# Softplus of three batches: the rounding of 1 + w taken over one VectorE instruction in SBUF

## The chip, the cores and the metric

The kernel runs on one core of one Trainium2 chip. The metric is the device time of one execution in microseconds; every time below is in microseconds unless it is marked ns. The engines are named as in the profile: PE is TensorE's matrix multiply and PEld its weight load, DVE is VectorE, ACT is ScalarE, POOL is GpSimd, SP is SyncE, which here only issues DMAs.

## The reference

One block of a network: half a mixture-of-experts layer, a state-space layer, half a mixture-of-experts layer again, each behind a layer norm and added to its input. The change lies in the state-space layer:

```python
x_proj = x @ W_x.T                                  # x is the normed input, (4, 512, 256)
dt_x, Bm, Cm = jnp.split(x_proj, [R, R + N], axis=-1)
dt = jax.nn.softplus(dt_x @ W_dt.T + b_dt)
A = -jnp.exp(A_log)
dA = jnp.exp(jnp.einsum('bld,dn->bldn', dt, A))
dBx = jnp.einsum('bld,bln,bld->bldn', dt, Bm, x)
# scan over l: h = dA * h + dBx;  y = sum over n of h * C;  then y + x * D
```

All in float32, N = 16 states for each of 4 batches, 512 positions, 256 channels. The softplus of z is computed as max(z, 0) + log1p(w) with w = exp(-|z|). The kernel gets log1p(w) as ln(1 + w) + (w - ((1 + w) - 1)): the second term gives back what the rounding of 1 + w lost.

## The kernel before

Channels lie on the partitions in two blocks (k = 0, 1) and positions along the free axis, so a batch's dt is 128 x 2 x 512. The state-space layer is 64 steps of one state each (s = 16b + n, batch b and state n), and a step uses every engine once:

- ACT (`decay`, line 583, and `outer`, line 597): two exponentials of dt times a number, 128 x 511 each, into `da`, and that part of the outer product dt x B (128 x 256 for each quarter of the positions) that DVE does not do. `BY_DVE` says how many of the four quarters are DVE's: in batch 0 2 2 2 1 1 2 2 2 1 2 1 1 0 1 0 1 for n = 0 to 15, in batches 1 and 2 1 1 2 1 1 2 2 2 0 0 0 1 0 1 0 1.
- PE (`turn_dbx`, line 940): eight transposes into a pair of PSUM banks.
- DVE (`scan`, line 1317): one scan over 1,024 elements. Its inputs are `da` in SBUF and the PSUM pair. DVE's part of `outer` (line 1301) for state n + 2 stands ahead of scan n; its inputs are `dtx_t` in SBUF and B in PSUM.
- POOL (line 455): the product of the state `hs` and the broadcast row `c_sb`, both in SBUF, 1,024 elements, into one of two buffers `gs`. PE (`add`, line 956) then sums it into PSUM. POOL waits for the scan of its state and for the sum of the state two before.

The order on each engine is written out by hand; there is no planner. Each engine has its own queue and goes through it in order, and counting semaphores join them. ACT runs three steps ahead (`AHEAD`), over four buffers of `da` and `hs` (`RING`): `decay` of state s waits for scan s - 4.

The projection and softplus of batch b + 1 are spread between the steps of batch b. PE makes z in one PSUM bank T. ACT takes Abs and Relu of it with the bias (lines 565 and 566: `w_exp` and `dt_sb`), Exp of -|z| over both blocks (`project_exp`, line 570) and Ln of 1 + w (`project_ln`, line 577) into `log_w`, which is the tile `tt`. DVE computes for each block k the rounding (`project_w`: line 1272 makes (w + 1) - 1 in T, line 1274 makes w minus that in T) and then the sum (`project_dt`: line 1280 adds `log_w` and T into T, line 1282 adds `dt_sb` and T into `dt_sb`). In each pair the second instruction waits for the first. These pairs stand behind the scans n = 5, 6, 7 and 8 of batches 1 and 2, and behind n = 6, 7, 8 and 9 of batch 0, in the order w0, dt0, w1, dt1. Once both dt are there, PE transposes dt (line 925) and DVE multiplies it by x (`project_dtx`, line 1288, behind n = 10 and 12, one later in batch 0).

Behind its steps n = 5 to 8 of batches 1 and 2 (6 to 9 of batch 0) POOL also normalises one tile of 128 x 256 each (line 403, input in SBUF), and in step 3 (5 in batch 0) it makes the reciprocal deviations (lines 388, 389).

The first batch's softplus runs before the scan loop. It writes into two banks of its own, and the change leaves its arithmetic and order as they are. So the changed softplus is that of batches 1, 2 and 3, which lies in the scans of batches 0, 1 and 2.

Of the kernel before, what the change touches and what calls it, by code (L numbers as in the profile page):

```python
# [15 lines left out]
ALU = mybir.AluOpType  # L16
ACT = mybir.ActivationFunctionType
# [10 lines left out]
def macaron_kernel(nc, x, w_xT, w_dtT, b_dt, a_log, d_skip, router_w, gate_w, up_w, down_w,  # L28
# [42 lines left out]
    with ExitStack() as ctx:  # L71
# [3 lines left out]
        def sem(name):  # L75
            return ctx.enter_context(nc.semaphore(name))
# [142 lines left out]
        back_in = [sem(f"back_in{b}") for b in range(BATCH)]  # L219
        back_x = sem("back_x")  # L220
        a_ready = sem("a_ready")
        pj_all, pj_copy, pj_bt, pj_btc, pj_z, pj_abs, pj_max, pj_exp, pj_w, pj_rest, pj_ln, pj_sum, pj_dt, pj_tp, pj_dtx = (
            sem(f"pj_{s}") for s in ("all", "copy", "bt", "btc", "z", "abs", "max", "exp", "w", "rest", "ln", "sum", "dt", "tp",
                                     "dtx"))
        c_rows = sem("c_rows")
        c_in = [sem(f"c_in{u}") for u in range(RING)]
# [262 lines left out]
        def _(act):  # L489
# [71 lines left out]
            def project_abs(b, k):  # L561
                act.wait_ge(pj_z, KC * b + k + 1)
                if b > 0:
                    act.wait_ge(pj_rest, KC * b)
                nc.scalar.activation(w_exp[:, k], pj_bank(b, k), ACT.Abs, bias=b_sb[:, k:k + 1]).then_inc(pj_abs, 1)
                nc.scalar.activation(dt_sb[:, k, seq(b)], pj_bank(b, k), ACT.Relu, bias=b_sb[:, k:k + 1]).then_inc(pj_max, 1)

            def project_exp(b):
                act.wait_ge(pj_abs, KC * (b + 1))
                nc.scalar.activation(w_exp[:], w_exp[:], ACT.Exp, scale=-1.0).then_inc(pj_exp, 1)  # L570

            def project_ln(b):

                act.wait_ge(pj_exp, b + 1)
                if b > 0:
                    act.wait_ge(pj_sum, KC * b)
                nc.scalar.activation(log_w, w_exp[:], ACT.Ln, bias=1.0).then_inc(pj_ln, 1)

            def decay(s):
                if s >= RING:  # L580
# [32 lines left out]
            def scan(b):  # L613
                more = b + 1 < BATCH
                for n in range(N):
                    if b == 0 and n in (3, 4):
                        project_abs(1, n - 3)
                    if b == 0 and n == 4:
                        project_exp(1)
                    if b == 0 and n == 6:  # L620
                        project_ln(1)
                    if N * b + n + AHEAD < STATES:
                        ahead(N * b + n + AHEAD)
                    if not more and n - 1 in PIECES:
                        tanh_piece(PIECES.index(n - 1))
                    if b < 2 and n == 0:
                        ln_copy(1, 5 + b)
                    if b == 1 and n == 1:
                        ln_copy(1, 7)
                    if (b, n) in ((0, 1), (2, 0)):  # L630
                        project_copy(b + 1)
                    late = (2, 1, 0, 0)[b]
                    if 0 < b < BATCH - 1 and n in (1 + late, 2 + late):
                        project_abs(b + 1, n - 1 - late)
                    if 0 < b < BATCH - 1 and n == 3 + late:
                        project_exp(b + 1)
                    if 0 < b < BATCH - 1 and n == 4 + late:
                        project_ln(b + 1)
                    if b == 0 and n == 15:
                        project_copy(2)  # L640
                    if not more and 6 <= n < 6 + LT:
                        normalise(b - 1, n - 6)
                    turn = 13 if more else 10
                    if b > 0 and n in (turn, turn + 1):
                        ln_copy(2, 2 * (b - 1) + n - turn)
# [422 lines left out]
        def _(dve):  # L1068
# [196 lines left out]
            def project_w(b, k):  # L1265

                if k == 0:
                    dve.wait_ge(pj_exp, b + 1)
                    dve.wait_ge(pj_max, KC * (b + 1))
                elif b > 0:  # L1270
                    dve.wait_ge(pj_dt, KC * b + 1)
                nc.vector.tensor_scalar(pj_bank(b, k), w_exp[:, k], 1.0, -1.0, ALU.add, ALU.add).then_inc(pj_w, 1)
                dve.wait_ge(pj_w, KC * b + k + 1)
                nc.vector.tensor_tensor(pj_bank(b, k), w_exp[:, k], pj_bank(b, k), ALU.subtract).then_inc(pj_rest, 1)

            def project_dt(b, k):

                dve.wait_ge(pj_ln, b + 1)
                dve.wait_ge(pj_rest, KC * b + k + 1)
                nc.vector.tensor_tensor(pj_bank(b, k), log_w[:, k], pj_bank(b, k), ALU.add).then_inc(pj_sum, 1)  # L1280
                dve.wait_ge(pj_sum, KC * b + k + 1)
                nc.vector.tensor_tensor(dt_sb[:, k, seq(b)], pj_bank(b, k), dt_sb[:, k, seq(b)], ALU.add).then_inc(pj_dt, 1)

            def project_dtx(b, h):

# [18 lines left out]
            def scan(b):  # L1304
                more = b + 1 < BATCH
                for n in range(N):
                    s = N * b + n
                    if s + 2 < STATES:
                        outer(s + 2)
                    dve.wait_ge(sc_dbx, s + 1)  # L1310
                    dve.wait_ge(sc_da, KC * (s + 1))
                    if s >= RING:
                        dve.wait_ge(sc_g, s - RING + 1)
                    if s == 0:
                        dve.wait_ge(da_zero, 1)
                    flat = "p k t -> p (k t)"
                    nc.vector.tensor_tensor_scan(hs[:, s % RING].rearrange(flat), da[:, s % RING].rearrange(flat),  # L1317
                                                 DBX[s % 2][:, :, :].rearrange(flat), 0.0, ALU.mult, ALU.add).then_inc(sc_h, 1)
                    if b == 0 and n in (1, 2):
                        shared_result(0, 3, (n - 1,))  # L1320
                    if b == 0 and n == 5:
                        dve.wait_ge(back_x, BATCH)
                        stats_of(1, BATCH - 1)
                    if not more and n - 2 in PIECES:
                        hidden_piece(PIECES.index(n - 2))
                    if b > 0 and n == 1:
                        add_y(b - 1)
                    if b > 0 and n == 2:
                        dve.wait_ge(sc_x, KC * b)
                        stats_of(2, b - 1)  # L1330
                    if more and n == 4:
                        project_bt(b + 1)
                    late = int(b == 0)
                    if more and n in (5 + late, 7 + late):
                        project_w(b + 1, (n - 5) // 2)
                    if more and n in (6 + late, 8 + late):
                        project_dt(b + 1, (n - 6) // 2)
                    if more and n in (10 + late, 12 + late):
                        project_dtx(b + 1, (n - 10) // 2)

# [106 lines left out]
```

## Time and profile before

| | |
|---|---|
| median of 3 runs | 451.88 (450.79 to 455.43) |
| span of the profiled execution, first to last instruction | 460.6 |
| its granted TensorE clock, mean | 0.979 |
| DVE busy | 366.0 (79%), 600 instructions |
| ACT busy | 284.4 (62%), 537 instructions |
| POOL busy | 281.2 (61%), 215 instructions |
| PE busy | 392.2 (85%), 2540 instructions |
| first and last scan start | 145.4 and 339.3 |

The profile gives no time of the profiled execution other than its span; that is 8.7 longer than the median of the runs without a profile, and so is not one of them. In the timelines a line is one instruction, or several of one group ("x2"), with its start, its length and, in brackets, how long its engine had been idle and what ended that. The recorded lengths of DVE and ACT overlap a little: the distance from one start to the next is the cost of an instruction that waits for nothing.

### The profile page before, as it was taken

To read this page: it belongs to the slowest core of one execution; us is meant where nothing else is said; L and a number is where in the kernel's file an instruction comes from. 1 tells how busy PE (TensorE), PEld (TensorE's weight loads), DVE (VectorE), ACT (ScalarE), POOL (GpSimd) and SP (SyncE) were. 2 spreads that over 40 slices of the span, in tenths; PEclk is the share of its full clock that TensorE was granted. 3 is DMA by queue.
4 is the path that set the end of the run, shared out by engine and by line. 5 is a ranking of instruction groups with operands and counts; after the bars stand their busy time and mean duration, and the time that the engine had idled before them with its cause. 6 is when DMAs were issued, how large, how long until landed. Compare 5 with 4: busy or idle time off the path is not lost. (4 is left out here: it accounts for less than half of the span.)

```text
span 460.6 us, 8038 instructions
## 1 busy us (share of the span) xinstructions
PE 392.2 (85%) x2540; PEld 264.6 (57%) x2540; DVE 366.0 (79%) x600; ACT 284.4 (62%) x537; POOL 281.2 (61%) x215
## 2 busy tenths in 40 slices
PE   6899889899896878798779788869898998888895
PEld 5447344444455668677677686768874654333442
DVE  5598666563789999999999999999986975465663
ACT  2410645553168799999999999979932012454553
POOL 6206155543265697987999699969961024756543
PEclk9999999999999988998999889999999999999999
DMA  8976027211530222232233222332300725234311
GB/s 268 364 206 221 27 65 243 74 45 45 184 94 0 73 70 70 90 111 68 78 93 101 81 70 73 116 91 72 113 23 2 229 67 142 82 92 111 100 55 48
DMA packets 34393, 47.88 MB, mean 104 GB/s; under 512 B 4265, under 2 KB 23533, under 8 KB 34352
## 3 DMA queue, kind: packets, MB, share of 16 engines
q1 hardware_dynamic: 30208, 36.82, 25.3%
q0 software_dynamic: 4144, 10.54, 7.8%
q8 instruction: 22, 0.36, 0.3%
q14 instruction: 19, 0.16, 0.1%
HBM read 35.37 MB, written 13.29 MB: 106 GB/s over the span
## 5 line engine op out<-in xcount | busy, mean ns | idle before, releaser
L455 POOL TENSOR_TENSOR gs<-hs,c_sb 128x1024 f32<-128x1024 f32 x63 | 148.6, 2376 | 28.4 <-DVE hs L1317 16.3
L1317 DVE TENSOR_TENSOR_SCAN hs<-da,bank 128x1024 f32<-128x1024 f32 x64 | 145.2, 2276 | 0.6 <-PE bank L940 0.6
L940 PE MATMUL bank<-ident,dbx_t 128*128 128x128 f32 x512 | 72.3, 287 | 20.1 <-DVE hs L1317 13.1
L583 ACT ACTIVATE da<-dt_sb,a_neg 128x511 f32<-128x511 f32 x128 | 84.8, 713 | 3.7 <-DVE hs L1317 2.4
L597 ACT ACTIVATE dbx_t<-dtx_t,h_sb 128x256 f32<-128x256 f32 x190 | 82.2, 498 | 0.1
L940 PEld LDWEIGHTS bank<-ident,dbx_t 128*128 128x128 f32 x512 | 60.4, 147 | 30.8 <-DVE hs L1317 19.0
L956 PE MATMUL bank<-ident,gs 128*128 128x128 f32 x504 | 69.6, 284 | 6.9 <-POOL gs L455 5.3
L956 PEld LDWEIGHTS bank<-ident,gs 128*128 128x128 f32 x504 | 59.5, 146 | 11.2 <-POOL gs L455 8.9
L520 ACT ACTIVATE th<-bank,da 128x256 f32<-128x256 f32 x36 | 17.1, 474 | 55.2 <-PE bank L829 29.0
L790 PE MATMUL bank<-xnT,w_gu 128*128 128x512 f32 x112 | 50.2, 595 | 0.0
L411 POOL DMA_INDIRECT da<-rows,row_token x29 | 30.8, 1063 | 29.3 <-issue 29.3
L829 PE MATMUL bank<-w_gu,tt 128*128 x72 | 35.5, 616 | 11.9 <-ACT tt L525 9.3
L505 ACT ACTIVATE hs<-bank 128x512 f32<-128x512 f32 x14 | 8.4, 597 | 54.3 <-PE bank L790 48.9
L430 POOL DMA_INDIRECT token_out<-y_sb,row_token x18 | 19.4, 1076 | 33.3 <-DVE y_sb L1240 30.5
L1225 DVE SCALAR_TENSOR_TENSOR q_sb<-th,bank 128x256 f32<-128x256 f32 x36 | 15.1, 421 | 30.8 <-ACT th L520 24.5
L411 POOL DMA_INDIRECT da<-rows,row_half x14 | 15.1, 1076 | 36.2 <-DVE row_token L1196 27.2
L826 PE MATMUL bank<-w_gu,tt 128*32 x72 | 34.2, 598 | 2.8 <-ACT tt L525 1.4
L826 PE MATMUL bank<-dtx_t,tt 128*32 128x512 f32 x72 | 34.3, 598 | 0.0
L430 POOL DMA_INDIRECT out<-y_sb,row_token x18 | 19.5, 1084 | 24.2 <-DVE y_sb L1243 21.9
L790 PEld LDWEIGHTS bank<-xnT,w_gu 128*128 128x128 f32 x112 | 20.6, 190 | 22.1 <-issue 21.9
L525 ACT ACTIVATE tt<-bank 128x512 f32<-128x512 f32 (+1 forms) x40 | 22.1, 553 | 15.8 <-issue 7.5
L829 PEld LDWEIGHTS bank<-w_gu,tt 128*128 128x128 f32 x72 | 12.3, 189 | 27.6 <-issue 27.5
(172 smaller groups left out, 733.4 us busy)
## 6 DMA issues: line engine op xcount, KB each, us to landing
c_sb<-c_dram SPq DMA_DIRECT2D x64, 256.0 KB, 3.1
rows<-xn_no SPq DMA_DIRECT2D x8, 516.0 KB, 5.3
rows<-xn_no SPq DMA_DIRECT2D x1, 2064.0 KB, 8.8
x_sb<-in_x SPq DMA_DIRECT2D x4, 512.0 KB, 5.4
w_gu<-in_gate_w SPq DMA_DIRECT2D x2, 1024.0 KB
w_gu<-in_up_w SPq DMA_DIRECT2D x2, 1024.0 KB
w_dn<-in_down_w SPq DMA_DIRECT2D x2, 1024.0 KB
xn_no<-token_out SPq DMA_DIRECT2D x4, 512.0 KB, 5.4
```

Source lines behind the costliest of these rows:

```text
L411: nc.gpsimd.indirect_dma_start(out=xr[:, u, lo:hi], out_offset=None, in_=source, in_offset=bass.IndirectOffsetOnAxis(ap=row, axis=0), boun ...
L430: nc.gpsimd.indirect_dma_start(out=rows_back, out_offset=bass.IndirectOffsetOnAxis(ap=row_token[:, TILE[j]:TILE[j] + 1], axis=0), in_=y_sb ...
L455: nc.gpsimd.tensor_tensor(gs[:, s % 2], hs[:, s % RING], c_sb[:, s % RING].unsqueeze(1).to_broadcast([P, KC, L]), ALU.mult).then_inc(sc_g, 1)
L525: nc.scalar.activation(tt[:, (j + 1) % 2, lo:hi], T[:, lo * P:hi * P].rearrange("p (a t) -> p a t", t=P), ACT.Copy).then_inc(ff_tpc, 1)
L583: nc.scalar.activation(da[:, s % RING, k, 1:L], dt_sb[:, k, seq(s // N)][:, 1:L], ACT.Exp, scale=a_neg[:, k, s % N:s % N + 1]).then_inc(sc ...
L597: step = nc.scalar.activation(dbx_t[:, s % TURNS, i, :], dtx_t[:, b % 2, i, :], ACT.Copy, scale=b_t[:, b, i, n:n + 1])
L790: last = nc.tensor.matmul(shared_banks(r, b, fo)[h], w_gu[:, k, SHARED, h * F + fo * P:h * F + (fo + 1) * P], xnT[:, k, b * L:(b + 1) * L] ...
L826: last = nc.tensor.matmul(H[j % 2][part, :], tt[:, j % 2, 2 + k, part], gu_part(i, g)[:, k, :] if g else w, start=(k == 0), stop=(k == KC ...
L829: last = nc.tensor.matmul(H[j % 2][:, :], tt[:, j % 2, 2 + k], w, start=(k == 0), stop=(k == KC - 1))
L940: mm = nc.tensor.transpose(DBX[s % 2][:, k, i * P:(i + 1) * P], dbx_t[:, s % TURNS, i, k * P:(k + 1) * P], ident[:])
L956: mm = nc.tensor.matmul(YA[k][:, i * P:(i + 1) * P], products[:, k, i * P:(i + 1) * P], ident[:], start=(s % N == 0 and i == 0), stop=(s % ...
L1317: nc.vector.tensor_tensor_scan(hs[:, s % RING].rearrange(flat), da[:, s % RING].rearrange(flat), DBX[s % 2][:, :, :].rearrange(flat), 0.0, ...
```

## The change

For batches 1, 2 and 3:

- ACT gets one instruction more (`project_u`): Identity of `w_exp` with bias 1 over both blocks, 1,024 elements, into `log_w`. It stands right behind Exp.
- DVE makes the correction in one instruction over both blocks (`project_lost`, 1,024 elements): (`log_w` - 1) - w, written over `w_exp`. Both inputs are in SBUF. It replaces the four instructions of lines 1272 and 1274 and stands behind scan 5 (6 in batch 0).
- ACT's Ln reads `log_w` and writes it in place, and waits for that correction. It moves in the written order from n = 6 to n = 7 in batch 0, from n = 5 to 6 in batch 1 and from n = 4 to 6 in batch 2.
- The sums now are `log_w` minus `w_exp` and that plus `dt_sb`, each still two instructions a block with the second waiting for the first, but with both inputs and the output in SBUF. They stand behind the scans 7 and 8 (8 and 9 in batch 0).
- The semaphore `pj_w` now counts ACT's instruction, and `pj_lost` is new, for the first batch's first instruction.

```diff
--- before.py
+++ after.py
@@ -219,8 +219,8 @@
         back_in = [sem(f"back_in{b}") for b in range(BATCH)]
         back_x = sem("back_x")
         a_ready = sem("a_ready")
-        pj_all, pj_copy, pj_bt, pj_btc, pj_z, pj_abs, pj_max, pj_exp, pj_w, pj_rest, pj_ln, pj_sum, pj_dt, pj_tp, pj_dtx = (
-            sem(f"pj_{s}") for s in ("all", "copy", "bt", "btc", "z", "abs", "max", "exp", "w", "rest", "ln", "sum", "dt", "tp",
+        pj_all, pj_copy, pj_bt, pj_btc, pj_z, pj_abs, pj_max, pj_exp, pj_w, pj_lost, pj_rest, pj_ln, pj_sum, pj_dt, pj_tp, pj_dtx = (
+            sem(f"pj_{s}") for s in ("all", "copy", "bt", "btc", "z", "abs", "max", "exp", "w", "lost", "rest", "ln", "sum", "dt", "tp",
                                      "dtx"))
         c_rows = sem("c_rows")
         c_in = [sem(f"c_in{u}") for u in range(RING)]
@@ -561,7 +561,7 @@
             def project_abs(b, k):
                 act.wait_ge(pj_z, KC * b + k + 1)
                 if b > 0:
-                    act.wait_ge(pj_rest, KC * b)
+                    act.wait_ge(pj_sum, KC * b)
                 nc.scalar.activation(w_exp[:, k], pj_bank(b, k), ACT.Abs, bias=b_sb[:, k:k + 1]).then_inc(pj_abs, 1)
                 nc.scalar.activation(dt_sb[:, k, seq(b)], pj_bank(b, k), ACT.Relu, bias=b_sb[:, k:k + 1]).then_inc(pj_max, 1)
 
@@ -569,12 +569,20 @@
                 act.wait_ge(pj_abs, KC * (b + 1))
                 nc.scalar.activation(w_exp[:], w_exp[:], ACT.Exp, scale=-1.0).then_inc(pj_exp, 1)
 
+            def project_u(b):
+
+                act.wait_ge(pj_exp, b + 1)
+                act.wait_ge(pj_sum, KC * b)
+                nc.scalar.activation(log_w, w_exp[:], ACT.Identity, bias=1.0).then_inc(pj_w, 1)
+
             def project_ln(b):
 
-                act.wait_ge(pj_exp, b + 1)
-                if b > 0:
-                    act.wait_ge(pj_sum, KC * b)
-                nc.scalar.activation(log_w, w_exp[:], ACT.Ln, bias=1.0).then_inc(pj_ln, 1)
+                if b == 0:
+                    act.wait_ge(pj_exp, 1)
+                    nc.scalar.activation(log_w, w_exp[:], ACT.Ln, bias=1.0).then_inc(pj_ln, 1)
+                else:
+                    act.wait_ge(pj_rest, KC + b)
+                    nc.scalar.activation(log_w, log_w, ACT.Ln).then_inc(pj_ln, 1)
 
             def decay(s):
                 if s >= RING:
@@ -617,7 +625,8 @@
                         project_abs(1, n - 3)
                     if b == 0 and n == 4:
                         project_exp(1)
-                    if b == 0 and n == 6:
+                        project_u(1)
+                    if b == 0 and n == 7:
                         project_ln(1)
                     if N * b + n + AHEAD < STATES:
                         ahead(N * b + n + AHEAD)
@@ -634,7 +643,8 @@
                         project_abs(b + 1, n - 1 - late)
                     if 0 < b < BATCH - 1 and n == 3 + late:
                         project_exp(b + 1)
-                    if 0 < b < BATCH - 1 and n == 4 + late:
+                        project_u(b + 1)
+                    if 0 < b < BATCH - 1 and n == 6:
                         project_ln(b + 1)
                     if b == 0 and n == 15:
                         project_copy(2)
@@ -1267,19 +1277,30 @@
                 if k == 0:
                     dve.wait_ge(pj_exp, b + 1)
                     dve.wait_ge(pj_max, KC * (b + 1))
-                elif b > 0:
-                    dve.wait_ge(pj_dt, KC * b + 1)
-                nc.vector.tensor_scalar(pj_bank(b, k), w_exp[:, k], 1.0, -1.0, ALU.add, ALU.add).then_inc(pj_w, 1)
-                dve.wait_ge(pj_w, KC * b + k + 1)
+                nc.vector.tensor_scalar(pj_bank(b, k), w_exp[:, k], 1.0, -1.0, ALU.add, ALU.add).then_inc(pj_lost, 1)
+                dve.wait_ge(pj_lost, k + 1)
                 nc.vector.tensor_tensor(pj_bank(b, k), w_exp[:, k], pj_bank(b, k), ALU.subtract).then_inc(pj_rest, 1)
 
+            def project_lost(b):
+
+                dve.wait_ge(pj_w, b)
+                nc.vector.scalar_tensor_tensor(out=w_exp[:], in0=log_w, scalar=1.0, in1=w_exp[:],
+                                               op0=ALU.subtract, op1=ALU.subtract).then_inc(pj_rest, 1)
+
             def project_dt(b, k):
 
                 dve.wait_ge(pj_ln, b + 1)
-                dve.wait_ge(pj_rest, KC * b + k + 1)
-                nc.vector.tensor_tensor(pj_bank(b, k), log_w[:, k], pj_bank(b, k), ALU.add).then_inc(pj_sum, 1)
+                if b == 0:
+                    dve.wait_ge(pj_rest, k + 1)
+                    total = pj_bank(b, k)
+                    nc.vector.tensor_tensor(total, log_w[:, k], pj_bank(b, k), ALU.add).then_inc(pj_sum, 1)
+                else:
+                    dve.wait_ge(pj_rest, KC + b)
+                    dve.wait_ge(pj_max, KC * (b + 1))
+                    total = log_w[:, k]
+                    nc.vector.tensor_tensor(total, total, w_exp[:, k], ALU.subtract).then_inc(pj_sum, 1)
                 dve.wait_ge(pj_sum, KC * b + k + 1)
-                nc.vector.tensor_tensor(dt_sb[:, k, seq(b)], pj_bank(b, k), dt_sb[:, k, seq(b)], ALU.add).then_inc(pj_dt, 1)
+                nc.vector.tensor_tensor(dt_sb[:, k, seq(b)], total, dt_sb[:, k, seq(b)], ALU.add).then_inc(pj_dt, 1)
 
             def project_dtx(b, h):
 
@@ -1331,10 +1352,10 @@
                     if more and n == 4:
                         project_bt(b + 1)
                     late = int(b == 0)
-                    if more and n in (5 + late, 7 + late):
-                        project_w(b + 1, (n - 5) // 2)
-                    if more and n in (6 + late, 8 + late):
-                        project_dt(b + 1, (n - 6) // 2)
+                    if more and n == 5 + late:
+                        project_lost(b + 1)
+                    if more and n in (7 + late, 8 + late):
+                        project_dt(b + 1, n - 7 - late)
                     if more and n in (10 + late, 12 + late):
                         project_dtx(b + 1, (n - 10) // 2)
 
```

## Rows read from the trace of the kernel before

**Rows 1.** Busy time by window (start:end; PE, PEld, DVE, ACT, POOL busy, clock, DMA).

```profile
160.00:180.00 20.00, 15.57 (x101) 14.24 (x100) 19.37 (x26) 19.92 (x35) 16.95 (x11) 0.83 0.24 71
210.00:225.00 15.00, 11.54 (x88) 11.20 (x89) 14.90 (x15) 14.94 (x26) 13.63 (x9) 0.89 0.25 79
```

**Rows 2.** Groups of instructions from 140 to 340 us, by line.

```profile
L455 POOL TENSOR_TENSOR gs<-hs,c_sb 128x1024 f32<-128x1024 f32 x63 | 148.6, 2376 | 28.4 <-DVE hs L1317 16.3 <-PE bank L956 11.5
L1317 DVE TENSOR_TENSOR_SCAN hs<-da,bank 128x1024 f32<-128x1024 f32 x64 | 145.2, 2276 | 0.6 <-PE bank L940 0.6
```

**Rows 3.** Timeline of DVE, behind scans 5 to 8 of batch 1 (start, length).

```profile
216.34 0.67 DVE L1272 TENSOR_SCALAR bank<-w_exp 128x512 f32<-128x512 f32 x1
217.65 2.28 DVE L1317 TENSOR_TENSOR_SCAN hs<-da,bank 128x1024 f32<-128x1024 f32 x1
219.85 0.67 DVE L1280 TENSOR_TENSOR bank<-tt,bank 128x512 f32<-128x512 f32 x1
220.56 0.69 DVE L1282 TENSOR_TENSOR dt_sb<-bank,dt_sb 128x512 f32<-128x512 f32 x1
221.16 2.28 DVE L1317 TENSOR_TENSOR_SCAN hs<-da,bank 128x1024 f32<-128x1024 f32 x1
228.18 0.41 DVE L1301 TENSOR_TENSOR dbx_t<-dtx_t,bank 128x256 f32<-128x256 f32 x1
228.51 4.46 DVE L1317 TENSOR_TENSOR_SCAN hs<-da,bank 128x1024 f32<-128x1024 f32 x2
```

**Rows 4.** Timeline of ACT, the same stretch.

```profile
213.16 1.07 ACT L570 ACTIVATE w_exp<-w_exp 128x1024 f32<-128x1024 f32 x1
214.11 1.34 ACT L583 ACTIVATE da<-dt_sb,a_neg 128x511 f32<-128x511 f32 x2
217.07 1.28 ACT L577 ACT_TABLE_LOAD   x1
218.36 1.06 ACT L577 ACTIVATE tt<-w_exp 128x1024 f32<-128x1024 f32 x1
```

**Rows 5.** Timeline of POOL, the same stretch.

```profile
214.60 2.37 POOL L455 TENSOR_TENSOR gs<-hs,c_sb 128x1024 f32<-128x1024 f32 x1
217.34 2.37 POOL L455 TENSOR_TENSOR gs<-hs,c_sb 128x1024 f32<-128x1024 f32 x1 [0.37 <-PE bank L956]
219.69 1.24 POOL L403 TENSOR_SCALAR xn_no<-x_sb,mv,rstd 128x256 f32<-128x256 f32 x1
220.87 2.39 POOL L455 TENSOR_TENSOR gs<-hs,c_sb 128x1024 f32<-128x1024 f32 x1
```

**Rows 6.** Instructions of line 1346 (min/median/max ns); POOL's timeline beside them.

```profile
L1346 DVE TENSOR_TENSOR dbx_t<-hs,c_sb x2: 678/968/1258, 341.6 to 342.8; 128x512 f32<-128x512 f32 x2
...
340.00 2.35 POOL L455 TENSOR_TENSOR gs<-hs,c_sb 128x1024 f32<-128x1024 f32 x1 [0.78 <-PE bank L956]
```

**Rows 7.** Instructions of line 1259.

```profile
L1259 DVE TENSOR_TENSOR x_sb<-xn_no,x_sb x3: 1212/1224/1225, 118.8 to 128.9; 128x1024 f32<-128x1024 f32 x3
```

**Rows 8.** Instructions of lines 604 and 583, the latter's table loads.

```profile
L604 ACT ACTIVATE xn_no<-x_sb,mean_rstd,rstd x4: 590/596/605, 318.7 to 328.4; 128x256 f32<-128x256 f32 x4
...
L583 ACT ACT_TABLE_LOAD  x3: 1283/1283/1283, 171.9 to 264.9; - x3
```

**Rows 9.** Timelines of DVE and POOL, batch 0 (scans 6, 10) and batch 2 (scans 5, 9).

```profile
165.20 2.28 DVE L1317 TENSOR_TENSOR_SCAN hs<-da,bank 128x1024 f32<-128x1024 f32 x1
180.90 2.28 DVE L1317 TENSOR_TENSOR_SCAN hs<-da,bank 128x1024 f32<-128x1024 f32 x1
...
163.08 4.69 POOL L455 TENSOR_TENSOR gs<-hs,c_sb 128x1024 f32<-128x1024 f32 x2
...
263.59 2.27 DVE L1317 TENSOR_TENSOR_SCAN hs<-da,bank 128x1024 f32<-128x1024 f32 x1
277.95 4.45 DVE L1317 TENSOR_TENSOR_SCAN hs<-da,bank 128x1024 f32<-128x1024 f32 x2
...
265.27 2.36 POOL L455 TENSOR_TENSOR gs<-hs,c_sb 128x1024 f32<-128x1024 f32 x1 [1.24 <-PE bank L956]
```

## The prediction

> **What bounds the kernel now.** I read the busy time by window first, since the change lies in three stretches of the scan loop. In all three DVE and ACT are busy nearly throughout, and POOL for much of the time [rows 1]. Two full engines are not two bounds, so the second view is the groups of instructions in the scan loop, with what each engine waited for [rows 2]: DVE's 64 scans were preceded by 0.6 us of idle time in all, while POOL waited 28.4 us in front of its products, most of it for a scan. DVE sets the pace; an instruction added to it or taken from it moves the end of the loop one to one. ACT is full but ahead: the reader sees in ACT's timeline that exponentials of state n + 3 are made while DVE is at scan n or before. The third view is the timeline of DVE, ACT and POOL side by side, behind scan 5 of batch 1 [rows 3 to 5]; the fourth is any place in the trace where DVE reads two SBUF tiles while POOL works [rows 6]. There is just one. None of DVE's instructions in the stretches that the change touches does that now: each has one input in PSUM, and the changed ones have none.
>
> **What DVE is spared.** The rounding pair costs from its start to the next scan 217.65 - 216.34 = 1.31 us [rows 3], and goes twice a batch: 2.62. In its place comes one instruction over 1,024 elements from SBUF. The nearest row is line 1259, two SBUF inputs, 1,024 elements, POOL idle or nearly: 1.22 us, of which 0.08 overlaps the next (a scan of 2.28 is followed after 2.20) [rows 3, 7]: 1.14. Saved: 1.48 a batch, 4.4 in all. The sum pairs stay two dependent instructions of 512 elements each, now 1.31 too [rows 3]; the quicker of the two instructions of line 1346 took 0.678, against 0.67 and 0.69 here [rows 6, 3], so SBUF in place of PSUM gives nothing.
>
> **What ACT gets.** Identity over 1,024 elements costs what Exp does from its start to the next, 214.11 - 213.16 = 0.95 us [rows 4]. It needs no table load: at line 604 Identity runs four times between exponentials, and no load follows the one at 264.9 [rows 8]. The two loads around Ln stay as they are. Three times 0.95 lies beside DVE's work. If that cover were gone, it would be 2.9 us.
>
> Ln moves behind one more state of ACT's work in batch 1. One state costs 217.07 - 214.11 = 2.96. So Ln's load starts at 214.11 + 0.95 + 2 x 2.96 = 220.98, and Ln ends 1.29 + 1.06 later, at 223.33 [rows 4]. I keep the clock of the old trace in this walk. The exponentials and outer product of state 10 then come at 223.33 + 1.29 + 2.96 = 227.6, and scan 10 started at 230.7 (half of the double scan at 228.51) [rows 3], so they stay in time.
>
> **What DVE waits for now.** The row that decides is the last product's [rows 6]. Of two equal instructions of line 1346, 512 elements, both inputs in SBUF, one took 0.678 us and the other 1.258. The long one was the first, at 341.6 (had it been the second, at 342.8, POOL would have been done); POOL's product ran from 340.00 to 342.35. 341.6 + 1.258 = 342.9, so it ended some 0.54 after POOL's end, its 0.678 less a start of 0.14. I read it as: DVE's instruction stood until POOL's was through. By the Trainium skill, "SBUF — State Buffer", section "Who interferes with whom", a VectorE instruction with two SBUF inputs contends with a GpSimd instruction that reads SBUF, because the second input comes through a read port that the two share, and whichever comes second stands until the other is finished; this row agrees, and no other row here shows it.
>
> The change makes five such instructions a batch: the correction and two pairs. POOL is then working through products (2.35 from start to start) and tiles (1.18) without a gap [rows 5]. The walk for batch 1, with grants at the end of what POOL runs, 0.54 of DVE's work per 512 elements, and 0.08 of overlap:
>
> - Scan 5 ends at 216.34 [rows 3]. POOL's product runs to 216.97 [rows 5]. The correction runs from there to 218.04, scan 6 from 217.97, scan 7 from 220.17 to 222.37.
> - POOL stands for the correction: product 5 from 218.04 to 220.39, tile 0 to 221.57, product 6 to 223.92.
> - DVE stands at sum 0: for Ln until 223.36, then for POOL until 223.92. It is through at 224.45. Its second half waits for the first's semaphore and starts only 0.03 after its recorded end (219.85 + 0.67 to 220.56) [rows 3]. POOL has been standing, and takes its tile in between: 225.63. The second half ends, and scan 8 starts at 226.09, where it started at 224.67 (a scan and a pair behind 221.16).
> - Scan 8 ends at 228.29, product 7 at 228.51; sum 1 from there, POOL's tile to 230.22, second half, next instruction at 230.68. The outer product takes 0.33 (228.18 to 228.51) [rows 3]; scan 9 starts at 231.01 and not at 228.51. **Batch 1: +2.5.**
>
> The same walk in batch 0: scan 6 ends at 167.40, POOL's products end at 167.77 [rows 9], so the correction waits 0.4; the sums wait for Ln and a product, for a tile, for a tile, and the last second half for a whole product. Scan 10 starts at 185.1 and not at 180.90: **+4.2.** In batch 2 scan 5 ends at 265.79, where POOL's product of 265.27 has just begun and runs to 267.63 [rows 9]: the correction waits 1.8, and the sums as in batch 1. Scan 9 at 281.7 and not at 277.95: **+3.7.** (These are net: the rounding pairs are gone from the walk.) Together +10.4 us. Nothing behind takes it back, as DVE has no idle time to give up [rows 2]; PE and ACT wait for scans more than now, which costs nothing. The sum is on a span of 460.6, which is 8.7 over the median. The loop is the same work in both, so I add it to the median: 451.9 + 10.4 = 462.3.
>
> **Bounds of the unknown cost.** The wait for POOL has one row, 0.58 us. Below, it is nothing, if that row has another reason. Above, each of 15 instructions waits a whole product, 2.35, for 35 us; POOL would run out of scans to work on long before, and I take 12 us beyond the forecast as the end. The walk has 0.6 to 2.4 a wait, between both, and nearest the row.
>
> **Rivals.**
>
> *The pair is not parted.* POOL may not get in between the halves of a sum; then only the correction and the first halves wait, nine instructions. The walk becomes +1.0, +1.6 and +2.8, in all +5.3: 457.2. For it speaks that the gap between the halves is only 0.03 long; against it, that POOL stands ready and DVE has to ask anew. By the skill's same page, section "A bandwidth-pool intuition that's wrong", blocked GpSimd work came about 115 ns after VectorE's end; no row here shows this, and by it the pair would stay whole.
>
> *No waiting for POOL (not slower).* If DVE's second SBUF input meets nothing, only the arithmetic is left. It saves 4.4, but Ln is late: DVE reaches sum 0 of batch 1 at 216.34 + 1.14 + 2 x 2.20 = 221.88 and stands until 223.36. That takes back 1.5 there, 0.7 net in batch 0 (where it now waits 0.3), and 0.1 in batch 2. The end is 2.1 to 2.3 earlier: 449.8. For it speaks that one row carries the other side. Against it, that row ends where POOL's end puts it, to about 0.05 us. The sign turns where the 15 waits come to under 2.1 us together, 0.14 each.
>
> *The logarithm is early as well.* If ACT keeps its lead (a little less work in its states), the full 4.4 stays: 447.5. ACT's row is against it: it was 14.94 of 15 us busy [rows 1].
>
> *POOL goes first more than once.* With two POOL instructions ready, DVE may be passed over, and each wait takes one instruction more, 1.8 on average. With 15 of them 26 us; POOL empties its work sooner, so half, some 12: 474. No row speaks for it, as POOL had nothing queued at line 1346.
>
> **Chances.** Forecast 0.45; pair not parted 0.25; no waiting 0.17; early logarithm 0.04; passed over 0.09. A measurement tells about 1% (4.5 us) from no change. Over 456.4 lie the forecast, the last rival and 0.15 of the first: 0.69. Within: the other 0.10 of it and the no-wait case: 0.27. Faster: 0.04. The range of the forecast alone is 458 to 466 (each batch's last wait may meet a product or a tile, 1.2 either way, in three batches). To leave out no more than 2 in 10 it goes to 450 and 467, as the lower rival has 0.17 at 449.8, half of it inside.
>
> **What would show it.** Right: lines 1272 and 1274 only in the first batch; the correction's three instructions near 1.1 us each plus a wait inside their recorded length, or POOL's products beside them longer than the 2.39 of now [rows 5]; the second halves of the sums well over 0.7, by about 1.2 or 2.4; first scan to last scan 10 us longer, with scans still 2.28. Pair whole: first halves long, second halves 0.69. No waiting: all five at 1.22 and 0.69, and idle time of DVE in front of sum 0, ended by ACT's line of Ln. Wrong altogether would be scans, outer products or ACT's exponentials of another length, or a table load at the Identity.

## The result: 1.4% slower

The changed kernel took 460.14 us (median; 457.58 to 461.82, 16 runs), the kernel before beside it 453.39 (450.79 to 457.12, 16 runs). The ratio is 1.0137 (1.0111 to 1.0163), which on 453.39 is 6.2 us more, between 5.0 and 7.4 (the two medians lie 6.75 apart). The forecast was 462.3, 10.4 above the kernel before, with a range of 450 to 467; it had the side and the main mechanism, and made the loss 1.7 times too large.

First the page of the changed kernel: span, busy times, and the two groups that answer to [rows 2].

```profile
span 458.2 us, 8029 instructions
...
PE 394.5 (86%) x2540; PEld 267.1 (58%) x2540; DVE 369.4 (81%) x591; ACT 288.9 (63%) x540; POOL 286.5 (63%) x215
...
L455 POOL TENSOR_TENSOR gs<-hs,c_sb 128x1024 f32<-128x1024 f32 x63 | 149.8, 2391 | 29.3 <-DVE hs L1338 17.4
L1338 DVE TENSOR_TENSOR_SCAN hs<-da,bank 128x1024 f32<-128x1024 f32 x64 | 144.9, 2274 | 3.0 <-PE bank L950 3.0
```

This profiled span is 2.4 shorter than that of the kernel before, though the kernel is slower. The reason lies outside the scan loop, where both kernels do the same: that part took 266.6 us in the profile before and 258.9 in this one. So the two spans are not to be set against each other. What compares is the scan loop, from the start of the first scan to that of the last: 339.3 - 145.4 = 193.9 us before, 344.4 - 145.1 = 199.3 now, 5.4 longer. DVE has nine instructions less and is busy 3.4 us longer. Its scans, once held up for 0.6 us in all, now are held up for 3.0.

The second view is the instructions of the changed lines, one line at a time: shortest, median, longest in ns.

```profile
L1287 DVE SCALAR_TENSOR_TENSOR w_exp<-tt,w_exp x3: 1443/1675/2933, 167.2 to 268.6; 128x1024 f32<-128x1024 f32 x3
...
L1301 DVE TENSOR_TENSOR tt<-tt,w_exp x6: 719/916/2010, 176.4 to 280.9; 128x512 f32<-128x512 f32 x6
...
L1303 DVE TENSOR_TENSOR dt_sb<-tt,dt_sb x6: 851/932/932, 178.3 to 281.9; 128x512 f32<-128x512 f32 x6
L1303 DVE TENSOR_TENSOR dt_sb<-bank,dt_sb x2: 691/691/691, 137.9 to 139.2; 128x512 f32<-128x512 f32 x2
```

The last two rows are the same source line: with one input in PSUM (first batch) it takes 0.69, with two in SBUF, beside a tile of GpSimd, 0.93. Then DVE and POOL side by side behind scan 5 of batch 2, the counterpart of [rows 9].

```profile
268.62 2.93 DVE L1287 SCALAR_TENSOR_TENSOR w_exp<-tt,w_exp 128x1024 f32<-128x1024 f32 x1
...
275.85 2.01 DVE L1301 TENSOR_TENSOR tt<-tt,w_exp 128x512 f32<-128x512 f32 x1
277.89 0.93 DVE L1303 TENSOR_TENSOR dt_sb<-tt,dt_sb 128x512 f32<-128x512 f32 x1
```

```profile
268.10 2.37 POOL L455 TENSOR_TENSOR gs<-hs,c_sb 128x1024 f32<-128x1024 f32 x1 [1.25 <-PE bank L966]
270.67 3.10 POOL L455 TENSOR_TENSOR gs<-hs,c_sb 128x1024 f32<-128x1024 f32 x1 [0.20 <-PE bank L966]
...
274.95 2.37 POOL L455 TENSOR_TENSOR gs<-hs,c_sb 128x1024 f32<-128x1024 f32 x1
277.30 1.66 POOL L403 TENSOR_SCALAR xn_no<-x_sb,mv,rstd 128x256 f32<-128x256 f32 x1
```

The correction starts at 268.62 beside a product that ends at 270.47. It ends at 271.55, 1.08 behind that: 1,024 elements. The next product is recorded from 270.67 and takes 3.10 and not 2.37, as it stands for the correction. The same with the first half of the sum: it starts at 275.85, POOL's product ends at 277.32, it ends at 277.86. The tile recorded at 277.30 takes 1.66 and not 1.22. The second half, from 277.89, takes 0.24 over 0.69, and ends at 278.83, 0.13 before the tile does (278.96). So it did not stand for the whole tile. Of the 15 instructions one met nothing: the first half at 181.69 started just ahead of a tile and took 0.72.

**Where the 5.4 us are.** Recorded work of DVE for the three softplus: before, lines 1272, 1274, 1280 and 1282, six each, 0.672 + 0.696 + 0.677 + 0.691 us, 16.4 in all; now 6.05 + 7.35 + 5.51 = 18.9 (three times 2.02, six times 1.23, six times 0.92). 2.5 more, where undisturbed lengths of 1.2 and 0.69 would have made 11.9. Waits for TensorE: 2.4 more, in batch 0. Waits for Ln: 0.7 more. Sum 5.6, less 0.4 for which `add_y` of batch 0 (it adds a finished batch's y to x, behind scan 17) waited before and does not now: 5.2.

The 2.4 were not in the forecast. TensorE's rows in batch 0, first before, then in the changed kernel:

```profile
167.15 1.06 PE L940 MATMUL bank<-ident,dbx_t 128*128 128x128 f32 x8 [2.31 <-issue]
168.05 1.44 PE L956 MATMUL bank<-ident,gs 128*128 128x128 f32 x8
```

```profile
168.00 1.94 PE L950 MATMUL bank<-ident,dbx_t 128*128 128x128 f32 x8 [3.40 <-DVE hs L1338]
```

TensorE stood for 3.40 us and not 2.31, as ScalarE's outer product came 1.1 later, counted from the start of scan 6, behind the Identity. Then its eight transposes took 1.94 and not 1.06: the lower of its two clocks (1.2 and 2.4 GHz), right behind that idle time; before, the clock fell a little later. So scans 7 and 8 waited.

The Identity and the longer stand are not enough for that. The same rows in two of the runs below, first with the Identity alone, then with one instruction for both blocks (whose program is the changed kernel's up to scan 8):

```profile
166.04 1.06 PE L950 MATMUL bank<-ident,dbx_t 128*128 128x128 f32 x8 [3.40 <-DVE hs L1327]
```

```profile
166.36 1.06 PE L950 MATMUL bank<-ident,dbx_t 128*128 128x128 f32 x8 [3.40 <-DVE hs L1340]
```

TensorE stood for 3.40 us in both and then went on at the full clock; in the second its granted clock was 1.00 from 159 to 179 us, against 0.83 from 160 to 180 in the changed kernel. The scans of these two loops stood idle for 0.6 and 0.8 us in all. In the run with all five in PSUM the clock fell right behind that stand again, and its scans waited 2.0. So the 2.4 belong to where the clock fell in the one execution that was profiled. Without them the loop is about 3 us longer than before. What made the clock fall there, and how many of the 16 runs have it, is open.

### The profile page after: what moved, and what is told of

Read it like the earlier page. It is cut to its first block and busy times, and to the rows that moved or that the text cites. A ratio compares the mean times of both kernels' runs of the same rounds, so it can differ in the third digit from the quotient of the medians.

```text
span 458.2 us, 8029 instructions
## 1 busy us (share of the span) xinstructions
PE 394.5 (86%) x2540; PEld 267.1 (58%) x2540; DVE 369.4 (81%) x591; ACT 288.9 (63%) x540; POOL 286.5 (63%) x215
## 5 line engine op out<-in xcount | busy, mean ns | idle before, releaser
L950 PE MATMUL bank<-ident,dbx_t 128*128 128x128 f32 x512 | 73.9, 291 | 29.0 <-DVE hs L1338 25.9
L966 PE MATMUL bank<-ident,gs 128*128 128x128 f32 x504 | 68.4, 281 | 2.4 <-POOL gs L455 1.6
L800 PE MATMUL bank<-xnT,w_gu 128*128 128x512 f32 x112 | 51.5, 607 | 0.0
L430 POOL DMA_INDIRECT out<-y_sb,row_token x18 | 19.3, 1074 | 16.4 <-issue 8.4
L494 ACT ACTIVATE xnT<-bank 128x512 f32<-128x512 f32 x24 | 13.9, 589 | 20.8 <-PE bank L728 20.8
```

The source lines that it names most:

```text
L430: nc.gpsimd.indirect_dma_start(out=rows_back, out_offset=bass.IndirectOffsetOnAxis(ap=row_token[:, TILE[j]:TILE[j] + 1], axis=0), in_=y_sb ...
L800: last = nc.tensor.matmul(shared_banks(r, b, fo)[h], w_gu[:, k, SHARED, h * F + fo * P:h * F + (fo + 1) * P], xnT[:, k, b * L:(b + 1) * L] ...
L950: mm = nc.tensor.transpose(DBX[s % 2][:, k, i * P:(i + 1) * P], dbx_t[:, s % TURNS, i, k * P:(k + 1) * P], ident[:])
L966: mm = nc.tensor.matmul(YA[k][:, i * P:(i + 1) * P], products[:, k, i * P:(i + 1) * P], ident[:], start=(s % N == 0 and i == 0), stop=(s % ...
```

## The experiments

Each is read by its ratio to the kernel before, run on the same chip, and by the length of its scan loop. The diffs are cut: semaphores, most waits and what only follows from the lines shown are left out. Theory "port" is the forecast's; its rival puts the loss on ScalarE. The runs with later tiles, with the outer product, with the second half freed and with 1 + w in PSUM shared a slower chip, where the kernel before took 465.0; their ratios are to that. It has no profile there, so their loops are set against loops of other chips. What makes that chip slower lies in the main outside the loop: 268 to 272 us in these four profiles, 257 to 259 in the other experiments'.

**All five instructions with one input in PSUM.** The edit, from the changed kernel:

```diff
-nc.vector.scalar_tensor_tensor(out=w_exp[:], in0=log_w, scalar=1.0, in1=w_exp[:], op0=ALU.subtract, op1=ALU.subtract)
+nc.vector.scalar_tensor_tensor(out=w_exp[:], in0=T.unsqueeze(1).to_broadcast([P, KC, L]), scalar=0.0, in1=w_exp[:], op0=ALU.mult, op1=ALU.subtract)
-nc.vector.tensor_tensor(total, total, w_exp[:, k], ALU.subtract)
+nc.vector.scalar_tensor_tensor(out=total, in0=T, scalar=0.0, in1=w_exp[:, k], op0=ALU.mult, op1=ALU.add)
-nc.vector.tensor_tensor(dt_sb[:, k, seq(b)], total, dt_sb[:, k, seq(b)], ALU.add)
+nc.vector.scalar_tensor_tensor(out=dt_sb[:, k, seq(b)], in0=T, scalar=0.0, in1=dt_sb[:, k, seq(b)], op0=ALU.mult, op1=ALU.add)
```

> The changed kernel, but each of the five VectorE instructions of a batch takes the bank T in PSUM (times zero) in place of one of its two SBUF inputs; order, waits, sizes, ScalarE's Identity and the place of Ln stay. So the log term is left out of dt for batches 1 to 3. Loop below is first scan start to last scan start: 193.9 us before, 199.3 in the changed kernel. Theory 'port' (VectorE's two-SBUF instructions and GpSimd's stand for one another): the correction falls to about 1.2 us (mean 2.0 now), the sums to 0.69 (1.23 and 0.92 now), GpSimd's tiles back to 1.24; 7 us less recorded work, of which the late Ln and the wait for TensorE in batch 0 take back 1 to 3; loop 193 to 196, time within 0.5% of the kernel before. Rival 'late ScalarE' (the loss is the Identity and the later Ln): loop stays at 198 to 200, ratio 1.010 to 1.016.

Measured: 0.9983 (0.9951 to 1.0016), loop 195.8. The groups of the changed instructions and of POOL's tiles:

```profile
L1307 DVE SCALAR_TENSOR_TENSOR dt_sb<-bank,dt_sb 128x512 f32<-128x512 f32 x6 | 4.2, 692 | 0.2
L1301 DVE SCALAR_TENSOR_TENSOR tt<-bank,w_exp 128x512 f32<-128x512 f32 x6 | 4.0, 674 | 2.2 <-ACT tt L585 2.2
L1287 DVE SCALAR_TENSOR_TENSOR w_exp<-bank,w_exp 128x1024 f32<-128x1024 f32 x3 | 3.6, 1197 | 0.0
...
L403 POOL TENSOR_SCALAR xn_no<-x_sb,mv,rstd 128x256 f32<-128x256 f32 x15 | 18.3, 1221 | 0.0
```

As the theory "port" had it: the lengths fall to 1.20, 0.67 and 0.69, the tiles to 1.22, and the slowdown is gone, with ScalarE's Identity and the late Ln still in place. 2.5 of its 195.8 stand at scan 54 in batch 3, where the clock fell (below); in the three changed batches it is 0.7 quicker than the kernel before.

**Only the correction, only the sums.** The same edit, first line alone and last two alone.

> As the run before, but only the correction reads T in PSUM; the sums keep two SBUF inputs (dt's correction term is then w itself). Theory 'port': correction 1.2 us, three times 0.8 less than now, sums as now; loop about 197 (199.3 less 2.4, some of it taken back by waiting for Ln). Rival 'late ScalarE': 199.3.

> Only the sums read T in PSUM, the correction keeps two SBUF inputs (the log term is left out of dt). Theory 'port': first halves 0.69 in place of 1.23, second halves 0.69 in place of 0.92, together 4.7 less; loop 194 to 196. Rival 'late ScalarE': 199.3.

Measured: sums in PSUM 1.0010 (0.9973 to 1.0047), loop 194.1, as expected. Correction in PSUM 1.0156 (1.0098 to 1.0214, four runs), loop 203.6: a miss. With less asking for the port it did not lose less, and the profiled loop is 4.3 longer than the changed kernel's. Its second halves show why:

```profile
L1303 DVE TENSOR_TENSOR dt_sb<-tt,dt_sb x6: 932/2727/2787, 173.2 to 282.7; 128x512 f32<-128x512 f32 x6
```

Four of the six take 2.7 us. The correction no longer holds a product of POOL up (by 0.7 in the row of 3.10 above), so POOL is elsewhere when the sums come. In those four a product was recorded from before the second half began, and the half ended 0.55 behind it; at the other two it was a tile. The first of the four, at 173.23, ended at 175.95, its product at 175.40.

**GpSimd's tiles later.** That was then tested by the order on POOL, from the changed kernel:

```diff
-                    if b == 0 and 6 <= n < 6 + LT:
-                        normalise(1, BATCH - 1, (n - 6,))
+                    if b == 0 and 10 <= n < 10 + LT:
+                        normalise(1, BATCH - 1, (n - 10,))
-                    if 0 < b < BATCH - 1 and 5 <= n < 5 + LT:
-                        normalise(2, b - 1, (n - 5,))
+                    if 0 < b < BATCH - 1 and 9 <= n < 9 + LT:
+                        normalise(2, b - 1, (n - 9,))
```

> The changed kernel with GpSimd's normalised tiles taken out of the stretch: four steps later (behind the products n = 9 to 12, 10 to 13 in batch 0). Behind a first half of a sum GpSimd then has a product ready and no tile. The second halves took 0.93 beside a tile (0.69 alone) in the changed kernel, and 2.14 on average in the run with only the correction moved to PSUM. Theory 'a pair is parted by what GpSimd has ready, for as long as that one reads': second halves of 2.3 to 2.8 where a product is ready, loop 3 to 9 us longer than 199.3, although GpSimd has less to do there. Rival 'the pair stays whole, 0.93 is a fixed cost of two SBUF inputs in a dependent instruction': second halves 0.93 or 0.69, loop at 199 or below, since GpSimd's queue is shorter.

Measured: 1.0427 (1.0367 to 1.0487), loop 362.0 - 149.6 = 212.4, 13 more than the changed kernel, beyond the upper end. 4.9 of them are `add_y` waiting behind scans 17, 33 and 49 for the sums of POOL's later products. At the softplus the second halves are 10.9 longer and the first 1.8 shorter; the rest goes the other way, in shorter waits for TensorE and Ln. The instructions of line 1303, then DVE's and POOL's timelines at the first pair in batch 1:

```profile
L1303 DVE TENSOR_TENSOR dt_sb<-tt,dt_sb x6: 2730/2742/2753, 181.9 to 295.9; 128x512 f32<-128x512 f32 x6
```

```profile
233.91 0.90 DVE L1301 TENSOR_TENSOR tt<-tt,w_exp 128x512 f32<-128x512 f32 x1
234.84 2.75 DVE L1303 TENSOR_TENSOR dt_sb<-tt,dt_sb 128x512 f32<-128x512 f32 x1
```

```profile
229.07 7.97 POOL L455 TENSOR_TENSOR gs<-hs,c_sb 128x1024 f32<-128x1024 f32 x3 [0.55 <-PE bank L966]
```

All six second halves take 2.74: 0.69 and 2.05 of waiting. In the rows above the third product ends at 237.04 and the second half at 237.59. The pair is parted each time, and the price is that of what POOL has ready: 2.05 for a product, 0.24 for a tile.

**The port alone, 50 times.** From the kernel before:

```diff
-                                        B_T[:, b, LT - mine:, n:n + 1]
+                                        b_t[:, b, LT - mine:, n:n + 1]
```

> The kernel before with one operand moved: VectorE's 50 outer products of the scan loop read B from its copy in SBUF (b_t) and not from PSUM, so each has two SBUF inputs; nothing else changes, the result is the same. The price of such an instruction beside GpSimd's products, 50 times and without any part of the change. Theory 'port': each waits for the rest of a GpSimd instruction, 0.5 to 2.3 us where one runs; mean length from 0.49 to 1.2 or more, loop from 193.9 to 220 to 270. Rival 'no port' (the single row at the last product had another reason, and the changed sums are long for something of their own): mean 0.49, loop 194.

Measured: 1.0492 (1.0407 to 1.0577, two runs), loop 365.7 - 147.4 = 218.3. One operand's place, with the same result, costs 24 us of the loop, of which 20.9 are in the recorded lengths of these instructions.

```profile
L1303 DVE TENSOR_TENSOR dbx_t<-dtx_t,h_sb x50: 394/660/3791, 144.2 to 360.0; 128x256 f32<-128x256 f32 x34, 128x512 f32<-128x512 f32 x16
```

The shortest is as short as before (0.39), the mean of the 50 is 0.90 and not 0.49. Mean and loop lie a little under what was expected. The longest is a case of its own:

```profile
301.81 3.79 DVE L1303 TENSOR_TENSOR dbx_t<-dtx_t,h_sb 128x256 f32<-128x256 f32 x1
```

```profile
300.63 4.68 POOL L455 TENSOR_TENSOR gs<-hs,c_sb 128x1024 f32<-128x1024 f32 x2
```

The first of the two products ended at 302.99, the second went on at once to 305.32, and VectorE's instruction ended 0.28 behind that. It is recorded from 301.81 on, during the first product, and the second went ahead of it. That is the forecast's rival "POOL goes first more than once": it exists, with a product once in these 50. None of the changed kernel's 15 shows it.

**The Identity alone.** From the kernel before, with `project_u` behind Exp in both places and Ln as it was:

```diff
+                nc.scalar.activation(log_w, w_exp[:], ACT.Identity, bias=1.0).then_inc(pj_u, 1)
```

> The kernel before with nothing but ScalarE's extra Identity behind Exp (its result is overwritten by Ln, which reads w as before). Theory 'port': ScalarE's 0.95 a batch costs only what it shows as waits of scans for TensorE (2.4 us more of them in batch 0 of the changed kernel, beside a lower granted clock): loop 194 to 197, ratio 1.000 to 1.006. Rival 'late ScalarE': most of the 5.4 us, loop 198 or more, ratio over 1.010.

Measured: 1.0040 (1.0008 to 1.0072), loop 197.9. Of its 3.9 us 2.5 stand at scan 54, the clock's (below). The ratio is in the theory's range; the loop is over it by 0.9 with the clock's part and inside it without. The rest is 1.4, mostly waits for Ln (1.9, from 0.3), and not, as expected, waits for TensorE (0.6, as before). ScalarE's 0.95 is thus not free: of its 2.9 about half shows.

**The second half freed.** From the changed kernel, `total = T`, the first half written there:

```diff
-                    total = log_w[:, k]
-                    nc.vector.tensor_tensor(total, total, w_exp[:, k], ALU.subtract).then_inc(pj_sum, 1)
+                    total = T
+                    if k > 0:
+                        dve.wait_ge(pj_dt, KC * b + k)
+                    nc.vector.tensor_tensor(total, log_w[:, k], w_exp[:, k], ALU.subtract).then_inc(pj_sum, 1)
```

> The changed kernel, but the first half of a sum writes T in PSUM and the second reads it there: the second halves have one SBUF input, the first halves still two. Result as the reference's. Theory 'port': second halves 0.69 (0.92 now), GpSimd's tiles held once and not twice; first halves and correction as now; loop 1 to 2 us under 199.3, ratio about 1.010. Rival 'parting costs nothing': 199.3.

Measured: 1.0143 (1.0061 to 1.0225), loop 200.4. A miss: the second halves fell to 0.69, but the first ones took 1.64 on average, from 1.23, and the corrections 2.25, from 2.02. The wait moved to other instructions, as POOL met DVE at another moment. (1.3 of the loop are the wait at scan 54.)

**One instruction for both blocks.** From the changed kernel, `tensor_tensor` over `log_w` and `w_exp[:]`, then over `log_w` and `dt_sb[:, :, seq(b)]`, both behind scan 7 (8 in batch 0).

> The changed kernel with both blocks of a sum in one instruction of 1,024 elements, behind scan 7 (8 in batch 0): three instructions with two SBUF inputs a batch and not five, still two of them a dependent pair. Less arithmetic: 3 x 1.14 against 1.14 + 2 x 1.31 is 0.34 a batch less. Theory 'what counts is how often VectorE asks for the port while GpSimd has something ready': each batch meets one wait for a product and one tile less, loop 196 to 198.5 (199.3 in the changed kernel), ratio 1.005 to 1.012. Rival 'what counts is the length for which the port is held': 199 to 201, since as many elements pass.

Measured: 1.0123 (1.0081 to 1.0165), loop 342.5 - 143.5 = 199.0, of which 1.2 stand at scan 54. With them it is in the rival's range and without them in the theory's, and the ratio is at the theory's upper end: this run does not tell the two apart. It is not better than the changed kernel either: that one's 199.3 hold 2.4 of waits for TensorE, and here there are next to none.

**1 + w in PSUM, a correct version.** From the kernel before, for both blocks in turn (ScalarE's line, then VectorE's in place of lines 1272 and 1274):

```diff
+                nc.scalar.activation(pj_bank(b, k), w_exp[:, k], ACT.Identity, bias=1.0).then_inc(pj_u, 1)
+                    nc.vector.scalar_tensor_tensor(out=T, in0=T, scalar=1.0, in1=w_exp[:, k], op0=ALU.subtract, op1=ALU.subtract)
```

> From the kernel before: ScalarE writes 1 + w of one block at a time into T (Identity, 512 elements, the first behind Exp, the second behind step 6), VectorE makes the correction in one instruction a block from T and w back into T, sums and Ln as before. No VectorE instruction has two SBUF inputs; VectorE is spared 6 instructions of 0.71 us. Theory 'port is all that spoiled the change': loop 4.2 less, of which waiting for ScalarE (full in these stretches; the kernel before with only the Identity added waited 1.6 us more for Ln and lost 1.5 net) takes back 1 to 3; loop 191 to 193, ratio 0.992 to 0.998. Rival 'ScalarE is the second bound': all 4.2 are taken back, loop 194 to 196, ratio 1.000 to 1.006.

Measured: 1.0034 (0.9995 to 1.0073), loop 195.9, of which 1.2 stand at scan 54. With or without them it is in the rival's range, and so is the ratio: the expectation under "port is all" fell. DVE is spared 4.2 us and waits for ScalarE and TensorE instead: 2.2 for the Identity, 1.8 for Ln, 1.8 for TensorE (0.6 before). ScalarE is the second bound.

**The same for the second block alone:**

> The attempt to beat the kernel before, from the run with 1 + w in PSUM, where ScalarE took back what VectorE was spared (4.0 us of waiting for Ln and the Identity). Only the second block gets its 1 + w from ScalarE, into T, behind step 6; the first block keeps VectorE's two instructions. VectorE is spared 3 x 0.71 = 2.1 us, ScalarE gets 3 x 0.57 and Ln stays where it is in the kernel before. Theory 'port and ScalarE, both': loop 191.8 to 193.5 (193.9 before), ratio 0.995 to 0.999, unless the clock's fall in batch 3 adds its wait for tanh (1.2 to 2.5 us in some runs). Rival 'ScalarE takes back any lead': loop 194 or more.

Measured: 1.0001 (0.9973 to 1.0030), loop 192.8, 1.1 us less, as expected; in whole runs it can't be told from no change, and the ratio is a little over what was expected. Nothing tried beats the kernel before.

## Why the forecast had the side and not the size

- **DVE sets the loop's pace**: right. 5.4 us more in the loop, 6.2 in the runs.
- **Five instructions a batch now stand for POOL** [rows 6]: right for 14 of the 15, and shown by the run with all five in PSUM, the run with the sums in PSUM and the outer product. By the Trainium skill, "SBUF — State Buffer", section "Who interferes with whom", whoever comes second stands until the other is finished; the changed kernel's rows agree for a correction behind a product (end 1.08 behind the product's). They do not for a second half behind a tile, which ended 0.13 before the tile's recorded end.
- **The correction waits 0.4, 0.6 and 1.8**: the three took 1.44, 1.68 and 2.93, that is 0.24, 0.48 and 1.73 over 1.2. Right.
- **"POOL has been standing, and takes its tile in between: 225.63"**: this is the step that was mis-sized. POOL does get in, but I charged the tile's 1.18 from start to start, and a whole product once. Measured: 0.24 a tile, no product, 1.4 us for all six in place of some 8. A tile's recorded length on POOL is not the time for which it keeps VectorE waiting. The forecast's own rows could not show it, since [rows 6] have only a product.
- **The rival "the pair is not parted"** was nearest in time (457.2 from 451.9, +5.3) for the wrong reason. The run with later tiles shows the pair parted six times of six. By the 115 ns that the Trainium skill, "SBUF — State Buffer", gives in its section "A bandwidth-pool intuition that's wrong" the pair would have stayed whole; with 0.03 between its halves it did not.
- **ScalarE's work is covered, Ln in time**: too good. Waits for Ln grew by 0.7, and the Identity alone cost 1.4 of a loop. I checked scan 10 of batch 1 and not scan 7 of batch 0, where TensorE stood longer behind the Identity. The 2.4 us of waiting there came only with the lower clock: two other runs had the same stand without it.
- By batch, from scan 6 to 10 (5 to 9): forecast +4.2, +2.5, +3.7; measured +2.6, +1.0, +2.3. With 0.24 in place of each tile and of the product the sum of +10.4 falls by 5 x 0.94 + 2.11 = 6.8 to 3.6, and the 2.4 make it 6.0, against 5.4. That the sums are so close is in part luck: by batch the same gives +3.6, +0.6 and +1.8, since each shift also changes which instruction of POOL the next one meets. The forecast's total, too, is nearer to the measured one than its steps, as 2.4 of the loop's 5.4 come from waits that it had at nothing.
- **"No waiting for POOL"**, the rival at 449.8, was too good even for a kernel that meets nothing: the run with all five in PSUM was at 0.9983 (0.9951 to 1.0016), which can't be told from no change. Its gain of 0.7 in the changed batches is less than the rival's 2.1, as scans waited 1.4 more for TensorE and sums 1.9 more for Ln.

Left open: what a sum would cost under other meetings of POOL and DVE. Three runs with nearly the same work on VectorE have loops of 199.3, 203.6 and 212.4 (4.9 of the last at `add_y`), depending on which POOL instruction is next. Open too: why a tile lets VectorE go so early.

## What to carry to other kernels

Count VectorE's SBUF inputs before moving an operand out of PSUM: an instruction that is shorter by itself can stand for GpSimd's. Think twice before splitting such work into dependent instructions, since GpSimd got in between the two here whenever it had something ready, and ask what it will have ready then. And work moved to an engine that is busy 99% of a stretch is not hidden, even if it is not the one that sets the pace.

## What the runs showed that I had not expected

- VectorE waits for much less than the recorded length of a GpSimd instruction where that is short: it loses 0.24 us beside a 1.22 us tile (128 x 256, one SBUF tile as input), but 2.05 beside a 2.37 us product (128 x 1,024, two). Since a half ends 0.55 behind a product, and the second half ended 0.97 behind the first (278.83 - 277.86), my estimate is that a tile is out of its way after some 0.4.
- Even a tiny one of GpSimd's stands: beside the correction in batch 0 the 128 x 4 instruction of line 388 took 1.05 us, where the median of the twelve is 0.20.
- TensorE's clock falls at different places in runs of nearly the same kernel. In batch 3, 305 to 325 us, it was granted in full in the kernel before and 0.83 with the Identity alone:

```profile
305.00:325.00 20.00, 16.47 (x131) 15.37 (x131) 19.86 (x26) 16.89 (x36) 16.46 (x11) 1.00 0.24 79
```

```profile
305.00:325.00 20.00, 16.96 (x112) 15.76 (x111) 17.56 (x23) 14.20 (x32) 14.78 (x10) 0.83 0.22 68
```

DVE then waits up to 2.4 us for a tanh behind TensorE's products. Nothing of the softplus is near. A loop's length from one profile carries 1 to 2.5 us of it, here or, as in the changed kernel, in batch 0.
